# Weights, statistics and projections moved in a two-layer Mamba, tree and expert kernel

## The reference

```python
x = L0_attn_x
xn = _layernorm(x)
x = x + _L0_attn_ref(xn, ...) + _L0_ffn_ref(xn, ...)
xn = _layernorm(x)
x = x + _L1_attn_ref(xn, ...) + _L1_ffn_ref(xn, ...)
```

```python
scores = softmax(xt @ Wr)
G, idx = top_k(scores.T, k)          # k = 1024 of 4096 rows for each expert
h = gelu(einsum('ekd,edh->ekh', xt[idx], W1) + b1)
X_e = einsum('ekh,ehd->ekd', h, W2) + b2
out = zeros.at[idx].add(G[..., None] * X_e)
```

## Time and profile before

| | before |
|---|---|
| median of three runs | 1580.8 us |
| profiled execution | 1576.46 us |
| its span | 1574.6 us |
| instructions | 22674 |
| mean granted TensorE clock | 0.961 |

### The profile page before, as it was taken

One profiled execution on the slowest core, in us unless ns is written; L12 is line 12 of the kernel. 1 busy time (PEld: TensorE's weight loads), 2 busy tenths in 40 slices (PEclk: granted clock), 3 DMA queues, 4 the chain that ended last, 5 costly groups with the idle time before them and its releaser, 6 DMA issues.

```text
span 1574.6 us, 22674 instructions
## 1 busy us (share of the span) xinstructions
PE 1453.0 (92%) x7315; PEld 1061.9 (67%) x7315; DVE 1079.9 (69%) x2557; ACT 727.3 (46%) x1468; POOL 533.4 (34%) x631
## 2 busy tenths in 40 slices
PE   4889999999999999998689888999889999999996
PEld 3556867676776768677345555455568888888895
DVE  4888686776868686842698888978854555546542
ACT  1443252525253443522456555656455555655552
POOL 1233424242424334241123222333334434534343
PEclk7999999999999999998799999999999999999998
DMA  6110120303020211200501111112023334433332
GB/s 215 54 55 27 38 84 1 121 0 107 13 94 27 76 44 40 68 9 33 177 17 67 46 55 64 61 45 68 24 86 78 72 85 102 101 76 67 86 52 27
DMA packets 71846, 100.90 MB, mean 64 GB/s; under 512 B 13000, under 2 KB 58192, under 8 KB 71760
## 3 DMA queue, kind: packets, MB, share of 16 engines
q1 hardware_dynamic: 59472, 82.77, 16.1%
q0 software_dynamic: 12288, 17.05, 6.4%
HBM read 74.30 MB, written 25.49 MB: 63 GB/s over the span
## 4 chain that ended last, share of the span: by engine, by line
PE 63%; issue 15%; DVE 10%; POOL 7%; ACT 2%; DMA 1%; SPq 0%; DVEq 0%; PEldq 0%; POOLq 0%; PEld 0%; ACTq 0%
PE bank L2081 59%; DVE u L1466 3%; POOL yb L938 2%; POOL Xs L930 2%; POOL ry L946 1%; PE bank L2191 1%; PE bank L2457 1%; PE bank L2159 1%; DVE am L1895 1%; POOL out L994 1%; DVE xo L1627 1%; PE bank L2288 1%; POOL ry L943 1%; PE bank L2135 0%; SPq L586 0%
## 5 line engine op out<-in xcount | busy, mean ns | idle before, releaser
L2036 DVE TENSOR_TENSOR aml<-m0big,amh 128x512 fp32r<-128x512 f32 x128 | 88.3, 690 | 176.8 <-ACT amh L1332 176.6
L994 POOL DMA_INDIRECT out<-EW,IDX x64 | 106.4, 1662 | 225.1 <-DVE EW L2021 210.5
L1327 ACT ACTIVATE m0big<-bank,eb 128x512 f32<-128x512 f32 x128 | 87.9, 687 | 162.7 <-PE bank L2081 147.3
L2081 PE MATMUL bank<-w2h,amh 128*128 128x256 f32 x512 | 147.9, 289 | 0.0
L2081 PE MATMUL bank<-w2h,aml 128*128 128x256 f32 x512 | 144.8, 283 | 0.0
L2081 PE MATMUL bank<-w2l,amh 128*128 128x256 f32 x512 | 144.7, 283 | 0.0
L2081 PE MATMUL bank<-EW,am 128*128 128x256 f32 x512 | 115.8, 379 | 0.0
L1111 ACT ACTIVATE am<-bank,b 128x512 f32<-128x512 f32 x64 | 44.0, 688 | 154.8 <-PE bank L2081 154.3
L2081 PEld LDWEIGHTS bank<-EW,am 128*128 128x128 f32 x512 | 97.2, 190 | 13.5 <-ACT am L1111 0.3
L2081 PE MATMUL bank<-xTh,w1h 128*128 128x512 f32 x256 | 102.7, 401 | 2.8 <-DVE w1l L2027 2.8
L2081 PEld LDWEIGHTS bank<-w2h,amh 128*128 128x128 f32 x512 | 97.6, 191 | 8.3 <-issue 5.8
(11 more groups left out here) (336 smaller groups left out, 3681.9 us busy)
## 6 DMA issues: line engine op xcount, KB each, us to landing
EW<-in_e_w SPq DMA_DIRECT2D x16, 1024.0 KB, 5.8
dA0b<-dA_d SPq DMA_DIRECT2D x16, 512.0 KB, 3.8
E<-dA_d SPq DMA_DIRECT2D x16, 512.0 KB, 5.4
m0big<-dA_d SPq DMA_DIRECT2D x16, 512.0 KB, 4.7
xin<-in_L_attn_x SPq DMA_DIRECT2D x8, 512.0 KB
xp<-in_L_attn_x SPq DMA_DIRECT2D x8, 512.0 KB, 3.8
rows_d<-xo SPq DMA_DIRECT2D x8, 512.0 KB, 3.0
x_d<-xb SPq DMA_DIRECT2D x8, 512.0 KB, 4.1
```

Source lines behind the costliest of these rows:

```text
L994: g.indirect_dma_start(out=out_rows, out_offset=bass.IndirectOffsetOnAxis(ap=IDX[:, 4 * u + c:4 * u + c + 1], axis=0), in_=ye[:, q, c, :], ...
L1327: a.activation(am2[:, j % 2, :], bank[j % 2][:, :], ACT.Gelu, bias=eb1[:, u // 2, j:j + 1]).then_inc(gelu_sig.sem, 1)
L2036: v.tensor_tensor(aml[:, j % 4, :], am2[:, j % 2, :], amh[:, j % 4, :], ALU.subtract).then_inc(am_low.sem, 1)
L2081: return t.matmul(out_, lhsT, rhs, start=first, stop=last)
```

## The change

- SyncE's list is put in another order and counts on four semaphores instead of one: the four tree weights (`w_fuse`), the norm weight with dt's and B/C's weights, dt's bias and A (`w_dt`), x's weights, the taps and two biases (`w_x`), then z's and the output weights, D and the gate norm (`w_late`). The same 17 loads; the 15 others follow as before.
- VectorE takes the statistics of the first rows before any weight, then scales dt's and B/C's weights, normalises the rows for TensorE, scales x's weights, normalises the rows for the residual, then copies the fused products, writes the rows of identities and scales the late weights. TensorE waits for the tree weights only, and for each group of scaled weights where it uses them. GpSimd's `rstd(0)` stands ahead of its addition of two biases.
- In the layer-1 mixer the next step's blocks 0, 1, 2 are projected and convolved in slot 0 and 3, 4 in slot 1; none in slot 2. The third of slot 0 stands behind the output projection (on VectorE behind `mixed1`).
- The threshold rounds stand in tiles 0, 2 and 3. The rounds 0 to 11 keep the threshold as a number in fp32, `thrf`: a comparison that sums its three results, and one multiply-add; round 11 converts it to the integer. Rounds 12 to 14 are as before.
- The barrier between mixer and experts is gone. The first expert's first conversions stand in tiles 29 to 31 (ScalarE `high_w1`, `high_w2`; VectorE `low_w1`, `low_w2`), and `low_tokens(0)` ahead of the last `mixed1`. TensorE turns the first tokens ahead of the last output projection. `gather(0)` is split: two loads ahead of the gating of tile 30, two behind it.
- Buffers are put in another order, with a pad, so that the weights' parts lie over nothing that the last tiles use.

```diff
-            for L, w, s in zip(LAYERS, W, (w_loaded, w_rest)):
...
+            square_load(woT, "treeoutT", w_fuse)
+            load(n1w[:, :], d["n1w"], w_dt)
+            square_load(w["dt"][:, :, :], "m0_wdt", w_dt)
+            square_load(w["bc"][:, :, :], "m0_wbc", w_dt)
+            load(w["dtb"][:, :], rows("m0_dtb", LAYERS[0].heads), w_dt)
+            load(w["A"][:, :], rows("m0_alog", LAYERS[0].heads), w_dt)
+            square_load(w["x"][:, :, :], "m0_wx", w_x)
...
+            rstd(0)
+            pool.wait_ge(w_x, 16 * W_X)
             g.tensor_tensor(b2[:, 0, :], b2[:, 0, :], b2[:, 1, :], ALU.add).then_inc(pool_prep, 1)
-            rstd(0)
+            pool.wait_ge(w_late, 16 * W_LATE)
...
+                if n + 2 == TILES1:
+                    gather(0, 0, 2)
                 gated1(*divmod(n, CH))
                 if n:
                     y_rms1(*divmod(n - 1, CH))
                 if n + 2 == TILES1:
-                    gather(0)
+                    gather(0, 2, 4)
...
+                elif n + 3 == TILES1:
+                    s1.x2.wait_ge(act, STEPS - 2, CH)
+                    high_w1(0, 0)
+                elif n + 2 == TILES1:
+                    high_w1(0, 1)
+                    high_w2(0, 0)
...
             v.memset(dAT0[:, 0:1], 0.0).then_inc(own, 1)
+            norm(0)
+            dt_weights()
+            layer_norm(LAYERS[0], sets[0], 0, x_weights)
+            fused_weights()
+            late_weights()
             dve.wait_ge(own, 2)
-            norm(0)
-            layer_norm(LAYERS[0], sets[0], 0)
...
+                if n <= EXACT:
+                    op(v.tensor_scalar(hits1[:, 0:3], CNT, float(CAP), 0.0, ALU.is_ge, ALU.add,
+                                       accum_out=thrf[:, 1:2]))
+                    op(v.scalar_tensor_tensor(out=thrf[:, 0:1], in0=thrf[:, 1:2], scalar=float(1 << (28 - 2 * n)),
+                                              in1=thrf[:, 0:1], op0=ALU.mult, op1=ALU.add))
+                    if n == EXACT:
+                        op(v.tensor_copy(thr1[:, :], thrf[:, 0:1]))
...
-                if c != 2 and i < 5:
-                    threshold(3 * i + c - c // 3)
+                if c != 1 and i < 5:
+                    threshold(3 * i + c - (c > 0))
...
-                if following and c == 2:
-                    conv1(i + 1, 4)
                 sums1(i, c)
                 if following and c < 2:
-                    conv1(i + 1, 2 * c)
-                    conv1(i + 1, 2 * c + 1)
+                    conv1(i + 1, 3 * c)
+                    conv1(i + 1, 3 * c + 1)
                 if n:
                     mixed1(*divmod(n - 1, CH))
+                if following and c == 0:
+                    conv1(i + 1, 2)
...
+                elif n == 30:
+                    low_w1(0, 0)
+                elif n == 31:
+                    low_w1(0, 1)
+                    low_w2(0, 0)
+            low_tokens(0)
             mixed1(STEPS - 1, CH - 1)
-            dve.drain().then_inc(phase, 1)
-            dve.wait_ge(phase, 8)
...
-            pe.wait_ge(w_loaded, 16 * W_FIRST)
+            pe.wait_ge(w_fuse, 16 * W_FUSE)
...
             rows_turned(LAYERS[0], sets[0], 0)
+            pe.wait_ge(prepped, PREPPED_DT)
             dt_of(LAYERS[0], sets[0], 0)
             in_proj(LAYERS[0], sets[0], 0, 0)
+            pe.wait_ge(prepped, PREPPED_X)
             in_proj(LAYERS[0], sets[0], 0, 1)
+            pe.wait_ge(prepped, PREPPED_FIRST)
...
-            y_turned1(STEPS - 1, CH - 1)
-            project1(STEPS - 1, CH - 1)
...
+            y_turned1(STEPS - 1, CH - 1)
             s1.t1.wait_ge(pe, STEPS, 0)
             tokens(0)
-            pe.drain().then_inc(phase, 1)
-            pe.wait_ge(phase, 8)
+            project1(STEPS - 1, CH - 1)
```

More of the change, by code:

```diff
@@ L41 @@
 LIM = -110.0
+EXACT = 11
 fp32 = mybir.dt.float32
@@ new lines, in _ @@
+            square_load(w["x"][:, :, :], "m0_wx", w_x)
+            load(w["conv"][:, :, :], d["m0_conv"], w_x)
+            load(b2[:, 0, :], rows("b2", D), w_x)
+            load(b2[:, 1, :], rows("treeb", D), w_x)
+            square_load(w["z"][:, :, :], "m0_wz", w_late)
+            load(w["D"][:, :], rows("m0_D", LAYERS[0].heads), w_late)
+            square_load(w["out"][:, :, :], "m0_wo", w_late)
+            load(w["gn"][:, :], d["m0_gn"], w_late)
+            square_load(w1, "w1", w_rest)
@@ L634, in store_back @@
+            load(v["A"][:, :], rows("m1_alog", LAYERS[1].heads), w_rest)
+            load(v["D"][:, :], rows("m1_D", LAYERS[1].heads), w_rest)
+            square_load(v["out"][:, :, :], "m1_wo", w_rest)
+            load(v["gn"][:, :], d["m1_gn"], w_rest)
             def store_back(b):
@@ L960, in _, with gather @@
                             ALU.add).then_inc(bias_steps.sem, 1)
-            def gather(u):
+            def gather(u, first=0, last=4):
                 q = u % 2
@@ L967, in gather @@
                 gcol_sig.wait_ge(pool, u - 2, 1)
-                for c in range(4):
+                for c in range(first, last):
                     g.indirect_dma_start(out=xg[:, q, c, :], out_offset=None, in_=rows_d,
@@ L1401, in _, with dt_weights, x_weights @@
-            assert count == PREPPED_FIRST, count
-            dve.wait_ge(prepped, PREPPED_FIRST)
-            dve.wait_ge(consts, 9 + NB + 1)
+            dve.wait_ge(consts, 9 + NB + 1)
+            def dt_weights():
+                dve.wait_ge(w_dt, 16 * W_DT)
+                for n in ("dt", "bc"):
+                    for k in range(KD):
+                        scale(W[0][n][:, k, :], n1w[:, k:k + 1])
+                assert count == PREPPED_DT, count
+            def x_weights():
+                dve.wait_ge(w_x, 16 * W_X)
+                for k in range(KD):
+                    scale(W[0]["x"][:, k, :], n1w[:, k:k + 1])
+                assert count == PREPPED_X, count
+                dve.wait_ge(a_exp, 1)
+                scale(W[0]["A"][:, :], -1.0)
@@ new lines, in fused_weights @@
+            def fused_weights():
+                nonlocal count
+                dve.wait_ge(fused_full, 1)
+                dve.wait_ge(pool_prep, 1)
+                for k in range(KD):
+                    v.tensor_copy(wg[:, k, :], BACK[k][:, 0:LEAVES]).then_inc(prepped, 1)
+                    v.tensor_tensor(wv[:, k, :], BACK[k][:, LEAVES:2 * LEAVES], b2[:, 0, :], ALU.add).then_inc(prepped, 1)
+                    count += 2
+                assert count == PREPPED_FUSED, count
+                dve.wait_ge(prepped, PREPPED_FUSED)
+                v.tensor_copy(ID0.rearrange("p (h t) -> p h t", h=4),
+                              ident[:, :].unsqueeze(1).to_broadcast([P, 4, P])).then_inc(own, 1)
@@ L1405, in rest_of_weights, with late_weights @@
+            def late_weights():
+                dve.wait_ge(w_late, 16 * W_LATE)
+                for k in range(KD):
+                    scale(W[0]["z"][:, k, :], n1w[:, k:k + 1])
+                out_weights(W[0])
+                assert count == PREPPED_FIRST, count
+                dve.wait_ge(prepped, PREPPED_FIRST)
             def rest_of_weights():
```

192 lines of the change are left out of this document (83 added, 109 removed).

## The result

The changed kernel takes 1551.8 us (median of 4 runs, 1551.1 to 1556.9) against 1578.4 us (1575.5 to 1583.1). The ratio is 0.984, with a 95% interval of 0.982 to 0.986; 1555.4 had been forecast. Its profiled execution took 1551.8 us, with a span of 1549.8 us where 1574.6 stood: 24.8 us less.

What follows compares the result with a forecast made beforehand. No single engine was taken as the bound: a chain of waits at the start, neither VectorE nor TensorE alone in the mixer. 16.4 + 0 + 8.0 = 24.4 us off 1579.8 gave 1555.4, range 1546 to 1566.

Steps and rivals of the forecast that it cites:

- The sum: Whole kernel: 16.4 for the start, 0 for the mixer and 8.0 for the passage make 24.4 us less.
- Start: Up to layer 0's first turned block: split loads and early statistics gain 16.4 us, or 14.2 if the clock is low.
- Layer 0 to the mixer: Layer 0's steady steps run the instructions of before; their length was left alone.
- Mixer: Layer-1 mixer: 0 us a step, between -2.1 and +1.3; in sum 0, between -9 and +6 us.
- The account of a step: One mixer step of four tiles, by engine: still 48 us, one TensorE pause of 3.6 us, then probably 6.8 us low clock.
- the two waits: Mixer, slot 0: VectorE waits for the inner product and ScalarE's first projection; these take the 2 us shorter rounds save.
- The Trainium skill's sentence: Mixer: GpSimd contends with VectorE instructions having two SBUF inputs; a round meeting Xs gains 0.4 us, otherwise 0.95.
- Passage: From mixer to experts: first expert product 6.7 us earlier, 1.3 more from the clock holding; 8.0, between 5.5 and 8.5.
- The clock did not hold by itself: Rival, mixer: a shorter TensorE pause keeps the clock up, slot 3 takes 9.0 instead of 11.1 us; 1546 us, chance 0.14.
- A second pause: Rival, mixer: VectorE falls behind in slot 1 too, a second pause takes the clock again; 1588 us, chance 0.03.
- The start gave what it should: Rival, start: loads or clock keep dt's product until 20 or later, gain 10 us instead of 16.4; 1562 us, chance 0.16.
- The end did too: Rival, passage: late gathers or conversions delay tiles 30 and 31, stretch stays 12.7 us; 1563.4 us, chance 0.05.

Runs made afterwards that it cites:

- a_slots: The changed kernel with projections and threshold rounds back in the slots of before, rounds still in float: 1555.3 us, ratio 0.985 to the kernel before.
- a_warm: The changed kernel with three unused TensorE products in each of the mixer's first five steps, ahead of tile 3's turned block: 1547.8 us, ratio 0.979 to before.
- a_gather: The changed kernel with all four gathers of the first unit behind tile 30's gating again: 1553.6 us, ratio 0.983 to the kernel before.
- a_int: The changed kernel with all 15 threshold rounds in integers, in the new slots: 1557.2 us, ratio 0.987 to the kernel before.
- a_warm2: The changed kernel with three unused TensorE products in each of the mixer's first five steps, ahead of tile 0's turned block: 1544.8 us, ratio 0.977 to before.
- b_start: The kernel before with the start's part alone (split loads, statistics first, weights scaled in four parts): 1560.4 us, ratio 0.990 to the kernel before.
- b_end: The kernel before with the passage alone (no barrier, gathers two and two, first expert's weights converted in tiles 29 to 31): 1569.1 us, ratio 0.995.
- a_statlate: The changed kernel with the first rows' statistics behind the scaling of dt's and B/C's weights: 1558.5 us, ratio 0.987 to the kernel before.
- b_mixer: The kernel before with the mixer's part alone (new slots and float rounds): 1577.9 us, ratio 0.999 to the kernel before.
- a_decwarm: The changed kernel with layer 0's decay store and loads issued first and two unused TensorE products in each of two pauses of layer 0's first step: 1552.3 us.
- a_dec2: The changed kernel with the store and first three loads of layer 0's decays ahead of the residual, x(1) and late weights: 1551.9 us, ratio 0.982 to before.
- a_fill: The changed kernel with unused TensorE products in mixer steps 1 to 5, layer 0's first step and last pass, and the mixer's entry: 1545.1 us, ratio 0.975.

## Why the prediction was right, point by point

**The sum.** The span fell by 24.8 us where 24.4 had been forecast, as 15.9 - 1.4 + 2.3 + 6.7 + 1.3. That it comes so near is in part luck: the 2.3 us of the mixer and the 1.4 lost ahead of it, both forecast as 0, and the start's 0.5 too few nearly cancel.

**Start, forecast 16.4.** 16.3 by layer 0's fourth tile, 15.9 by its last. The steps: the tree product at 7.68 (7.6 forecast), A landed at 9.56 (9.8), dt's product at 14.94 (16), dt read at 18.92 (19.7), most projections at the high clock, the first turned block at 35.59 (36 to 38). The gain there, 18.0, was above my 15.6 to 17.6. What I didn't have is the wait behind it, which leaves 15.3 us at the first Bs (39.48 against 54.73) and 16.2 at the first tile. I took the stores and loads behind the start as before; but SP reaches the decays' store with x(1), the residual and the late weights still in flight, and the store takes 6.8 us. The two errors cancel, and that is luck. So is the fourth tile in part: other kernels with the instructions of after up to there have it at 15.6 (a_slots), 16.2 (a_warm), 16.3 (a_gather), 17.0 (a_int) and 11.2 (a_warm2).

**Layer 0 to the mixer, forecast 0.** Here 1.4 us were lost, and I had left this stretch alone. It isn't the change's work. In the changed kernel the clock was 0.50 from 690.8 to 707.8 us; in b_start, with the same instructions there, for 13.7 us:

```profile
692.50:706.20 13.70, 8.33 (x29) 6.90 (x29) 4.93 (x19) 4.28 (x6) 2.78 (x4) 0.50 0.28 94
```

The kernels with a low stretch of 13.6 or 13.7 us at this place (before, b_start, b_end, a_int, a_statlate, a_gather, a_warm2) all take 100.3 to 100.5 us from the last tile to the first block. Those with 17.0 or 17.1 (after, b_mixer, a_slots, a_warm, a_decwarm) take 101.6 to 101.9. a_dec2 takes 99.2; it has 13.7 us here, and a second low stretch behind it was 13.6 us long instead of the 17.0 of after. a_fill has 10.3 and 3.4 us and takes 99.4. What decides between the lengths stays open.

**Mixer, forecast 0 between -9 and +6.** 2.3 us were gained. The four steps with all rounds, for which I had 0, gave -0.1, 0.4, 0.4 and 0.2 us from block to block (blocks counted as 886.53 is in the kernel before and 871.72 in after). The fifth gave 1.1; its low stretch lasted 3.4 us (from 1004.8) where that of before lasted 6.8 (from 1019.2). The last two gave 0.6 and 0.2, and behind the last of these blocks 0.5 were lost again. The account of a step was right in each of its parts: the pause (3.6 forecast, 2.91 found), the low clock behind it, 11.1 us to the next block, the first convolution 8.0 us after the block (8.1), the third one over at 16.4 (16.7), slot 1 at 29.5 (29.8), the state at 36.4 (36.9), the two waits. What the forecast didn't separate is what gives and what takes: the float rounds gave 2.2 us in the old slots (a_slots against before), the new slots nothing, since what they save beside Xs they lose in waits and in a second convolution that now meets Xs, which the prediction didn't have.

**The Trainium skill's sentence** on GpSimd and VectorE (GPSIMD Engine Reference, 1. Specifications) agrees with this trace: the multiply-add, with two SBUF inputs, took 0.16 us alone and 0.72 beside Xs. The forecast that most rounds would no longer meet Xs held as well: two of three.

**Passage, forecast 8.0.** 6.7 and 1.3, both to the tenth. Every kernel with this part but a_gather shows the 6.0 us that are left of the 12.7. That the 1.3 fits to the tenth is luck: the experts take 410.0 to 411.0 us in the kernels whose first products run at the high clock (b_end 411.0), 411.4 to 411.9 in those where they don't (before 411.6). a_gather prices one piece at 1.9 us where I had expected 2 to 2.5 of that run.

**The rivals.** The clock did not hold by itself, and a_warm2 shows that the price put on it was right: 8.1 us against the 9 of the prediction. A second pause didn't come. The start gave what it should. The end did too: the gathers and conversions don't delay tiles 30 and 31.

**From span to median.** By the profiled run I forecast 1552.1 us, and 1551.8 was found; I then moved it by the mean of three runs of before to 1555.4. With its fourth run the median of before is 1578.4, not the 1579.8 that I had started from, which is 1.4 of the miss of 3.6 us. The other 2.2 are the 26.7 us by which the medians differ, less the 24.4 of the forecast; the profiled executions differ by 24.7, and with runs that spread over 6 us that is within chance.

## What to carry to other kernels

Before shortening work on the engine that seems late, look for the pause it leaves on TensorE: here three useless products in each of five pauses of 2.9 us gave 8 us in the mixer. Twelve cheaper rounds gave 2.2 (in the old slots) to 4.7 (in the new ones), and the rearrangement of the five projections gave nothing. Test such a filling in the pause itself; one slot ahead of it, the trace shows 1.1 us in the mixer. And where an early phase is pulled forward, look in the queue for small transfers that now stand behind large ones.

## What the runs showed of the hardware

- A store of 16 KB took 1.4 us to land where nothing large was in flight (before, a_dec2) and 6.8 us behind three loads of 512 KB issued in the 3.2 us before it (after).
- A multiply-add on 128x1 in VectorE, 0.16 us alone, took 0.72 us where it met GpSimd's 128x512 product, and 0.99, 0.98 and 0.71 in a_slots; each of the four ended when that product did, within 0.02 us.
- The same instructions with the same pauses ahead of them (3.80 and 3.90 us) met 17.1 and 6.8 us at 1.2 GHz in two executions. A single trace can't price an edit of 4 us in such a stretch; it takes a second kernel with the same code there to see it.
- More granted clock is not more speed: a mean of 0.970 instead of 0.965, with the mixer's pauses filled, went with 7 us less in the median; 0.984 instead of 0.970, with the other pauses filled too, with no gain that the runs can tell.
